# Ternary feed-forward weights: made from six steps of one pair of heads to the next and kept in HBM, instead of in the last four pairs

## The reference

```
x1 = LN(x + attention over features (512 x 512 scores per batch))
a  = self and cross attention of x1: 8 groups, each with 2 query heads, 2 cross query heads,
     one key, one value head of 128; every head is layer-normed; projections on fp8-rounded inputs
x2 = x1 + a Wproj (on fp8-rounded inputs)
x3 = LN(x2)                                 # feed-forward input
wq(w) = clip(round(w / mean|w|), -1, 1)     # ternary, one mean for w_gate_up, one for w_down
aq(r) = round(r * 127 / max|r|)             # per row
h  = silu(aq(x3) wq(w_gate)) * (aq(x3) wq(w_up))          # scaled back by mean|w| and the row's scale
y  = LN(x3 + aq(h) wq(w_down))
```

## Time and profile before

| | us |
|---|---|
| median of 3 runs | 1898.07 |
| the runs | 1894.26 to 1898.26 |
| the profiled execution's own time | 1892.83 |
| its span, first to last instruction | 1891.0 |
| stage A, up to the first kT of stage B (ACT L767) | 423 |
| pairs 0 to 30, from there to the kT of pair 31 | 423 to 1645.8 |
| pair 31 and the entry of stage C, to the first gate product | 1645.8 to 1696.2 |
| stage C | 1696.2 to 1891.0 |

### The profile page before, as it was taken

The page is one execution under the profiler, slowest core; times in us unless marked ns, Lnnn a source line. Parts: engine busy times, 40 slices in busy tenths (PEclk is TensorE's granted clock), DMA queues, the critical chain, the costliest instruction groups (busy, mean ns, idle before and its releaser), DMA issues.

```text
span 1891.0 us, 32035 instructions
## 1 busy us (share of the span) xinstructions
PE 1786.9 (94%) x11024; PEld 1248.7 (66%) x11024; DVE 1441.9 (76%) x4621; ACT 1095.3 (58%) x2526; POOL 268.5 (14%) x417
## 2 busy tenths in 40 slices
PE   7999999559999999999999999999999999879998
PEld 3444444237777778777778787777878877644554
DVE  1153524277888888888888888888878988888997
ACT  1131313236667666676666766666656666667776
POOL 0000000011111111111121211111112121101121
PEclk9999999779999999999999999999999999989999
DMA  6000000111101110110100111011010102210000
GB/s 223 22 1 23 1 0 0 44 37 67 47 25 42 40 35 13 58 35 25 58 23 25 46 36 36 12 59 34 14 46 2 47 24 69 78 57 12 24 26 31
DMA packets 40447, 70.77 MB, mean 37 GB/s; under 512 B 2912, under 2 KB 21856, under 8 KB 39264
## 3 DMA queue, kind: packets, MB, share of 16 engines
q1 hardware_dynamic: 40288, 68.73, 11.1%
HBM read 63.47 MB, written 4.19 MB: 36 GB/s over the span
## 4 chain that ended last, share of the span: by engine, by line
PE 71%; DVE 15%; issue 8%; ACT 3%; POOL 3%; DMA 1%; POOLq 0%; SPq 0%; DVEq 0%; ACTq 0%
PE bank L366 17%; PE bank L422 15%; PE bank L476 10%; PE bank L532 8%; PE bank L571 5%; PE bank L496 4%; PE bank L607 3%; PE bank L482 3%; PE bank L455 3%; PE bank L449 1%; DVE nq L1077 1%; DVE nmx L1183 1%; ACT yb L822 1%; PE bank L540 1%; POOL rsC L1362 1%
## 5 line engine op out<-in xcount | busy, mean ns | idle before, releaser
L834 ACT ACTIVATE pr<-bank,nmx 128x512 f32<-128x512 f32 x256 | 174.8, 691 | 141.9 <-DVE nmx L1183 141.5
L422 PE MATMUL bank<-wqs,XQ 128*128 128x256 f16 x2048 | 248.3, 275 | 4.4 <-DVE x L1107 4.4
L476 PE MATMUL bank<-prT,KV 128*128 128x256 f32 x1024 | 244.6, 382 | 0.1
L532 PE MATMUL bank<-kT,qT 128*128 128x512 f32 x512 | 242.9, 597 | 0.7 <-ACT kT L767 0.7
L422 PEld LDWEIGHTS bank<-wqs,XQ 128*128 128x128 bf16 x2048 | 198.9, 99 | 44.9 <-issue 15.5
L476 PEld LDWEIGHTS bank<-prT,KV 128*128 128x128 f32 x1024 | 191.2, 192 | 52.1 <-issue 22.8
L1328 POOL TENSOR_TENSOR rdev<-gvar,cst 128x7 f32<-128x7 f32 x128 | 193.0, 1508 | 10.0
L822 ACT ACTIVATE yb<-bank,rsT 128x128 bf16<-128x128 f32 x512 | 146.2, 373 | 62.8 <-PE bank L482 62.8
L1326 POOL TENSOR_TENSOR gvar<-mvB,geps 128x7 f32<-128x7 f32 x128 | 28.8, 225 | 1041.6 <-DVE mvB L1067 1034.6
L1183 DVE TENSOR_REDUCE nmx<-bank 128x1 f32<-128x512 f32 x256 | 166.6, 680 | 10.5 <-PE bank L532 7.3
L571 PE MATMUL bank<-identf,pr 128*128 128x128 f32 x1024 | 152.1, 277 | 15.2 <-DVE pr L1087 14.8
(11 more groups left out here) (162 smaller groups left out, 3207.9 us busy)
## 6 DMA issues: line engine op xcount, KB each, us to landing
wst<-in_wcat SPq DMA_DIRECT2D x24, 512.0 KB, 3.9
wpst<-in_wproj SPq DMA_DIRECT2D x8, 1024.0 KB, 5.2
wa<-in_wgu SPq DMA_DIRECT2D x16, 512.0 KB, 3.6
xT<-in_xT SPq DMA_DIRECT2D x4, 1024.0 KB, 5.3
x<-in_x SPq DMA_DIRECT2D x4, 1024.0 KB, 12.2
wkx<-in_wkvx SPq DMA_DIRECT2D x8, 512.0 KB, 4.8
wa<-in_wdn SPq DMA_DIRECT2D x8, 512.0 KB, 3.6
wst<-in_wgu SPq DMA_DIRECT2D x4, 1024.0 KB, 5.1
```

Of the source, the lines that this page charges most:

```text
L422: ins = mm(dst, XQ[:, b, c, k, j * P:(j + 1) * P], w, start=(k == 0 and m == 0), stop=(k == KT - 1 and m == 1))
L476: mm(OB[:, 0:2 * P], KV[:, n % 2, t, P:2 * P], prT[:, st % 2, t, :, :].rearrange("p h s -> p (h s)"), start=(t == 0), stop=(t == ST - 1))
L532: mm(SB_[h][:], qT[:, h, st * P:(st + 1) * P], kT[:, :], start=True, stop=True).then_inc(s["scores_made"], 1)
L834: act_f(pr[:, h, :], SB_[h][:], ACT.Exp, bias=nmx[:, st, h:h + 1], accum_out=su[:, st, h:h + 1]).then_inc(s["exp_done"], 1)
```

## The change

- **The sums come first.** `SUMS` is one piece per step in steps 0 to 23, which are pairs 0 to 5. `sums_ready` and `means_ready` move from pairs 24 and 25 to pairs 6 and 7.
- **The ternary weights are made in 24 pieces of 128 x 1024**, at (b, st) = (1,1), (2,1), (2,3), (3,1), (3,3) of groups 2 to 6 (the last of these 25 places is left out). Each piece is loaded into `wa` (`load_tern`), scaled by ACT in place (`tern_scale`, formerly DVE's), rounded by ACT into the first half of `wa` (`tern_round`), clipped there by DVE one step later (`tern_clip`), and stored by SP to an HBM scratch (`store_tern`). There is one buffer: the next load waits for that store to have landed.
- **Pairs 28 to 31 have no ternary arithmetic.** SP fetches the scratch in three DMAs of 2 MB (`fetch_tern`) at pairs 28, 29 and 30, each when the projections that read its place in XQ are done. PE waits for the three at the entry of stage C.
- **The first rows of stage C are spread out.** `x_stats` comes at steps 117, 119, 122, 125 (`XSTAT`), `x_prepare` at 119, 121 and 126, `x_norm` at 118, 120, 123, `xi_out` at 120 and 125, `turn_x` at (31, 1) and (31, 2), `xt_out` at 125 and 126. POOL's `of_x` stands at the same steps as `x_stats`.
- In SP's list of a pair the loads of the output weights (`load_out`) come behind the pieces, and `load_context` ahead of them. The places of yo, hb and hT in stage C are moved so that rows written early don't overlap live buffers.

```diff
-NCH = 12
-TURN = {(28, 2): 0, (28, 3): 1, (29, 1): 2, (29, 2): 3, (29, 3): 4, (30, 1): 5, (30, 2): 6, (30, 3): 7,
-        (31, 0): 8, (31, 1): 9, (31, 2): 10, (31, 3): 11}
+SUMS = {i: i for i in range(NABS)}
+TURN = {16 * g + 4 * b + st: i for i, (g, b, st) in enumerate(
+    [(g, b, st) for g in range(2, NG - 1) for b, st in ((1, 1), (2, 1), (2, 3), (3, 1), (3, 3))][:NABS])}
+XSTAT = {4 * NB * NG + o: t for t, o in enumerate((-11, -9, -6, -3))}
...
+        scr_gu = nc.dram_tensor("tern_gu", (P, KT, 2 * F), BF16, kind="Internal").ap()
+        scr_dn = nc.dram_tensor("tern_dn", (P, FT, D), BF16, kind="Internal").ap()
...
+        wt = wa[:, 0:WABS // 2].bitcast(BF16)
...
+            def load_tern(i):
+                if i:
+                    sp.wait_ge(s["tern_stored"], 16 * i)
                 else:
+                    sp.wait_ge(s["abs_made"], NABS)
+                dst = wa[:] if i < NABS1 else wa[:].rearrange("p (k n) -> p k n", k=2)
+                sp.dma_start(dst, piece(gu_cols, dn_cols, i)).then_inc(s["tern_read"], 16)
+
+            def store_tern(i):
+                sp.wait_ge(s["tern_made"], i + 1)
+                src = wt[:] if i < NABS1 else wt[:].rearrange("p (k n) -> p k n", k=2)
+                sp.dma_start(piece(scr_gu, scr_dn, i), src).then_inc(s["tern_stored"], 16)
+
+            def fetch_tern(i):
+                if i == 0:
+                    sp.wait_ge(s["tern_stored"], 16 * NABS)
+                sp.wait_ge(s["proj_q_made"], 4 * (TT - 3 + i))
+                sp.wait_ge(s["proj_kv_made"], 3 * (TT - 3 + i))
+                if i < 2:
+                    sp.dma_start(wgu[:, 2 * i:2 * i + 2, :], scr_gu[:, 2 * i:2 * i + 2, :]).then_inc(tern_loaded[i], 16)
                 else:
+                    sp.dma_start(wdn[:], scr_dn).then_inc(tern_loaded[i], 16)
...
-            turn_x(1, 1)
-            pe.wait_ge(s["tern_made"], 8)
+            pe.wait_ge(tern_loaded[0], 16)
+            pe.wait_ge(tern_loaded[1], 16)
...
+            def tern_scale(i):
+                w = 0 if i < NABS1 else 1
+                if i == 0:
+                    act.wait_ge(s["winv_ready"], 1)
+                act.wait_ge(s["tern_read"], 16 * i + 16)
+                act_f(wa[:], wa[:], ACT.Copy, scale=winv[:, w:w + 1], bias=INT_ROUND).then_inc(s["tern_scaled"], 1)
+
+            def tern_round(i):
+                act.wait_ge(s["tern_scaled"], i + 1)
+                act_f(wt[:], wa[:], ACT.Copy, bias=-INT_ROUND).then_inc(s["tern_int"], 1)
...
+            def tern_clip(i):
+                dve.wait_ge(s["tern_int"], i + 1)
+                v.tensor_scalar(wt[:], wt[:], 1.0, -1.0, ALU.min, ALU.max).then_inc(s["tern_made"], 1)
...
-                    if (n, st) in TURN:
-                        c = TURN[n, st]
-                        if c:
-                            tern_clip(c - 1)
-                        tern_scale(c)
-                    if n == TT - 1 and st:
-                        x_prepare(st - 1, (st - 1) % 2)
-                    if n == TT - 1:
-                        x_stats(st)
+                    if T - 1 in TURN:
+                        tern_clip(TURN[T - 1])
+                    if T in (4 * TT - 9, 4 * TT - 7, 4 * TT - 2):
+                        x_prepare((4 * TT - 9, 4 * TT - 7, 4 * TT - 2).index(T), 1)
+                    if T in XSTAT:
+                        x_stats(XSTAT[T])
```

More of the change, by code:

```diff
@@ L214, in build @@
         s = {n: sem(n) for n in names}
-        chunk_loaded = [sem(f"chunk_loaded{i}") for i in range(2)]
+        tern_loaded = [sem(f"tern_loaded{i}") for i in range(3)]
         out_stored = [sem(f"out_stored{i}") for i in range(2)]
@@ L329, in _ @@
                     copy_vx((n + 1) // 2)
+                if b == 1 and g + 1 < NG:
+                    load_context(g + 1)
+                if TT - 4 <= n < TT - 1:
+                    fetch_tern(n - (TT - 4))
+                for T in range(4 * n, 4 * n + 4):
+                    if T in SUMS:
+                        if SUMS[T] + 1 < NABS:
+                            load_abs(SUMS[T] + 1)
+                        else:
+                            load_tern(0)
+                    if T in TURN:
+                        store_tern(TURN[T])
+                        if TURN[T] + 1 < NABS:
+                            load_tern(TURN[T] + 1)
                 if b == 0 and g + 1 < NG:
                     load_out(g + 1)
-                if b == 1 and g + 1 < NG:
-                    load_context(g + 1)
-                if n + 1 < NABS:
-                    load_abs(n + 1)
-                if n == TT - 5:
-                    load_chunk(0)
-                    load_chunk(1)
-                for st in range(ST):
-                    if (n, st) in TURN and TURN[n, st] + 2 < NCH:
-                        load_chunk(TURN[n, st] + 2)
                 if b < 3 and 3 * (g + 1) + b + 2 < 3 * NG:
@@ L532, in pair @@
                         mm(SB_[h][:], qT[:, h, st * P:(st + 1) * P], kT[:, :], start=True, stop=True).then_inc(s["scores_made"], 1)
-                    if n == TT - 1 and st == 3:
-                        turn_x(0, 0)
+                    if n == TT - 1 and st in (1, 2):
+                        if st == 1:
+                            pe.wait_ge(s["xs_sub"], TT)
+                        turn_x(st - 1, st - 1)
                     if st == 1:
@@ L670, in _ @@
             gate_up(0, 0, 3, True)
[L671 removed]
+            pe.wait_ge(tern_loaded[2], 16)
             pe.wait_ge(s["acc_done"], LT)
@@ L1170, in means_ready @@
                 own.sync()
-                own.do(v.reciprocal(winv[:], wsc[:]))
-                own.sync()
+                v.reciprocal(winv[:], wsc[:]).then_inc(s["winv_ready"], 1)
             def pair(g, b, first, last):
@@ L1328, in deviations @@
                 g.tensor_tensor(rdev[:], gvar[:], CPOW, ALU.pow).then_inc(s["stats_ready"], 1)
-            def pair(gr, b, first, last):
-                n = 4 * gr + b
-                nxt = not (last and b == 3)
-                for st in range(ST):
-                    T = 4 * n + st
-                    if nxt:
-                        deviations(4 * n + 4 + st)
-                    if n == NABS and st == 1:
-                        pool.wait_ge(s["abs_ready"], 1)
-                        g.partition_all_reduce(asum3[:], asum2[:], P, RADD).then_inc(s["absum_ready"], 1)
-            pool.wait_ge(s["yA_made"], ST * NB)
-            g.memset(VB[:], 0.0).then_inc(s["vx_cleared"], 1)
-            for j in range(4):
-                deviations(j)
-            for b in range(NB):
-                pair(0, b, True, False)
-            for gr in range(1, NG - 1):
-                for b in range(NB):
-                    pair(gr, b, False, False)
-            for b in range(NB):
-                pair(NG - 1, b, False, True)
             def deviation(slot, var, count, used, done):
@@ L1370, in of_y, with pair @@
                 deviation(1, s["varY_ready"], t + 1, s["yo_ready"], s["rstdY_ready"])
+            def pair(gr, b, first, last):
+                n = 4 * gr + b
+                nxt = not (last and b == 3)
+                for st in range(ST):
+                    T = 4 * n + st
+                    if nxt:
+                        deviations(4 * n + 4 + st)
+                    if T in XSTAT:
+                        of_x(XSTAT[T])
+                    if n == 6 and st == 1:
+                        pool.wait_ge(s["abs_ready"], 1)
+                        g.partition_all_reduce(asum3[:], asum2[:], P, RADD).then_inc(s["absum_ready"], 1)
+            pool.wait_ge(s["yA_made"], ST * NB)
+            g.memset(VB[:], 0.0).then_inc(s["vx_cleared"], 1)
+            for j in range(4):
+                deviations(j)
+            for b in range(NB):
+                pair(0, b, True, False)
+            for gr in range(1, NG - 1):
+                for b in range(NB):
+                    pair(gr, b, False, False)
+            for b in range(NB):
+                pair(NG - 1, b, False, True)
             NT = NB * ST
-            for t in range(4):
-                of_x(t)
             for t in range(NT):
```

77 lines of the change are left out of this document (27 added, 50 removed).

## The result

| | before | changed |
|---|---|---|
| median, us | 1898.11 (1894.26 to 1898.26, 4 runs) | 1880.65 (1879.04 to 1883.98, 4 runs) |
| ratio of the runs | | 0.9915, 95% interval 0.9897 to 0.9933 |
| profiled execution, us | 1892.83, span 1891.0 | 1880.79, span 1877.4 |

The change makes the kernel faster by 0.85%, 12.0 us between the two profiled executions and 17.5 between the medians. The forecast was 11.8, reckoned on the profiled executions and carried over to the medians.

A forecast was written before the change was run, and what follows sets the result against it. Stage B was taken as TensorE's, with DVE late in the last pairs because ternary work stands ahead. The terms -7.0 - 12.5 + 7.7 = -11.8 us gave 1886.3 us on the median, chance 0.60, range 1878 to 1900.

The forecast's parts named there:

- Pairs 29 and 30: Ternary chunks leave, first rows of stage C come in: excess 9.3 us falls to 2.3, gain 7.0.
- Pair 31 and the entry: End of stage B into stage C: PE's waits fall from 13.2 to 3.5 us, clock returns 2.8; gain 12.5.
- The pieces: 24 ternary pieces in the steady part, about 2.15 us of ACT each, together cost 7.7 us, between 0 and 18.
- (2, 3): Five pieces there: ACT's next exp comes 1.6 us later, PE waits for the scaled row; 0.75 each, 3.75 in all.
- (3, 3): Four pieces there: exp comes 1.5 us later, 0.75 goes through to qT; 0.75 each, 3.0 in all.
- (1, 1), (2, 1), (3, 1): Fifteen pieces in step 1: exp 0.85 us late but covered by DVE's layer norm; 0.07 each, 1.0 in all.
- Rival 1: The steady pieces are free, PE's stalls coming out of gaps it has anyway: 1878.6 us; chance 0.12.
- rival 2: Step 1 has no cover, fifteen more stalls of 0.75 us: 1896.6, no change to be seen; chance 0.14.
- Sums and the sum over the partitions: Doubled sums in pairs 0 to 5 cost zero; the partition sum, moved to pair 6, costs what it cost.
- Rivals 3 and 4: Both slower: stalls at step-3 pieces halve TensorE's clock, 1901.6 us, chance 0.08; slow stores delay loads, 1913, chance 0.06.
- Rival 4: One buffer, store and load in series: a 7 us store makes loads 3 us late at nine places; 1913; chance 0.06.
- The carry-over to the medians: The sum of -11.8 us, made on the profiled execution (1892.8 to 1881.0), applied to the median: 1898.1 to 1886.3.

The follow-up runs named there:

- x_in_31: Changed kernel with the first rows of stage C put back into pair 31, the pieces staying; 1885.28 us, ratio 0.9938.
- control_before: The kernel before, unchanged, run again; 1897.17 us (11 runs), ratio 1.000.
- no_pieces: Changed kernel without the ternary pieces of groups 2 to 6, scratch filled once from another tile, so weights are wrong; 1874.99 us, ratio 0.9888.
- reduce_at_3: Changed kernel with POOL's sum over the partitions in step 3 of pair 6 instead of step 1; 1878.04 us, ratio 0.9892.
- pieces_clear: Changed kernel with the (2, 3) pieces moved to pairs 7 and 28 to 30, clips of (3, 3) pieces deferred a step; 1886.01 us, ratio 0.9941.

## Why the prediction was right

Each of the three terms of the sum had the mechanism, and each was off in size. That the total came to -12.0 for -11.8 is luck: the three terms together measure -14.3, and the remaining rows of the table, put at nothing, bring them back by 2.3. The largest of these rows (the sum over the partitions, stage C, the time outside the span) differ by as much between runs of one kernel. Over the medians the change is worth about 16 us, so the forecast was some 4 us short.

- **Pairs 29 and 30**, forecast a gain of 7.0, measured 6.3. The waits at (30, 0) and (30, 3) came where they were put, 1.70 for 1.5 and 1.16 for 0.7. The excess was reckoned against 39.5 and 38.4; x_in_31 shows that in this last group the pairs take 39.26 and 38.13 without any such work. So the excess was 9.8 where 9.3 was reckoned, and what is left of it is 3.5 where 2.3 was forecast, all in pair 30 (39.25 and 41.64 us, kT to kT, for about 39.6 and 40.6). 1.7 of the old excess was a fall of the clock in pair 30, which the sum charged to the chunks; without it the gain is 4.6. `x_stats` at (29, 1), put at 0.1, costs nothing to be seen.
- **Pair 31 and the entry**, forecast 12.5, measured 13.7. Of the waits of the earlier trace rows 3.9 are left (forecast 3.5): 1.86 at the text transposition (forecast 1.9), 0.82 and 1.22 at `pr` (0.9 and 0.7), none for x. The part that was under-sized is the clock: 2.8 us were counted back, but the granted clock is 1.00 over the whole stretch where it was 0.90, and 13.7 less the 9.3 of the waits leaves 4.4. PE's busy time says the same: 31.66 us for the products that took 36.43. The sum had cut the 5.0 us of lost clock down by PE's busy share, and almost all of it had fallen on busy time. x_in_31 stands between: waits of 8.1 at `pr`, `px` and x, clock 0.92. In these three windows the clock is lower where the waits are longer; no run changed the clock alone, and pairs 29 and 30 of control_before show that the same waits don't always bring the same clock.
- **The pieces**, forecast 7.7, measured 5.7. (2, 3): 0.75 forecast, 0.93 measured, of which 0.80 is the wait at `pr` (1.10 for 0.30). (3, 3): 0.75 forecast, 0.27 measured, by no_pieces. Set against the same place there, the exp of pair 12's step 0 starts 1.4 us later (forecast 1.5), `yb` 0.55 and `prT` 0.24: ACT's gaps of 0.67 and 0.16, and instructions that follow each other closer once they needn't wait, take up nearly all, where the sum had left 0.75. (1, 1), (2, 1), (3, 1): 0.07 forecast, 0 measured, so the cover that the earlier trace rows shows for (2, 1) is there at all fifteen. Rival 1 (free) and rival 2 (no cover in step 1) are both refuted.
- **Sums and the sum over the partitions**: zero forecast, +0.2 and -1.1 measured. The second costs 4.97 in pairs 6 and 7 where it had cost 6.09, but 5.05 in control_before, so "costs there what it cost" holds. I did not ask whether that stall had to be at all, and reduce_at_3 shows that it hadn't.
- **Rivals 3 and 4**: the clock is 1.00 in every pair with a piece, behind five waits of 1.1 us; the stores land in 2.0 us and ACT never waits for a piece. Rival 4's mechanism is real (6.6 us in pieces_clear), but there it took a clip one step late.
- **The carry-over to the medians** gave 1886.3 where 1880.65 came. On the profiled execution the same sum gave 1881.0, measured 1880.79. The median of before was taken over long executions and the profiled one was short; against 11 and 23 further runs of before, with medians of 1897.17 and 1896.05, the difference is 15.4 to 16.5 us, of which the profiles show 12 (device time) to 14 (kT 1 to the end).

## What to carry to other kernels

A job that is moved from a crowded place into a steady loop costs what its neighbours on the same engine leave over in that one step. Here the same 2.25 us on ACT cost 0, 0.27, 0.93 or 1.60 us by its place, most where a weight split or a weight copy stood behind it; so list what else each step of the loop carries before spreading work evenly. When spreading, take off steps that double up, not merely those that look busy, and reckon the turn-around of a single buffer from the clip, not from the piece. And a stall that a change only carries along is worth a question of its own: one condition, `st == 3` for `st == 1`, took away a stall of 5 us between the marks (2.6 us in the medians).
